# A retention layer with 64 routed experts: results scattered by token from sixteen buffers, and two projection chunks moved ahead of the routing's one-hot products

## The chip, the cores and the metric

The kernel runs on one core of a Trainium2 chip. The metric is the device time of one execution in microseconds, the median of three runs: 293.25 us (291.96 to 296.66). A profiled execution, which took 291.93 us, gives the spans and rows quoted here.

## The reference, cut to what matters

The input x is 1024 tokens of 256 channels (2 sequences of 512). The output is the sum of x, a retention layer and a mixture of experts, both of them on the normalised input.

```python
xn = _layernorm(x)
# retention: 8 heads of 32, decays g; chunk by chunk with a state
q, k, v = xn @ Wq + bq, xn @ Wk + bk, xn @ Wv + bv
inner = (q k^T * D) v ;  cross = (q * g^(i+1)) S ;  S = g^C S + (k * g^(C-1-i))^T v
# experts: 64 of width 176, six for each token; two shared ones (width 352 together)
scores = softmax(xn @ gate_w.T); topk_w, topk_ids = top_k(scores, 6); topk_w /= sum(topk_w)
routed = sum over the six of topk_w * (silu(g) * u) @ w_down[e]
shared = (silu(sg) * su) @ ws_down
out = x + retention(xn) + routed + shared
```

## The kernel before, in words

**Names.** PE multiplies matrices, ACT, DVE and POOL work on elements, SP issues plain DMAs. POOL also issues the indirect DMAs, whose rows are given by a list of indices in SBUF. P is 128, T 1024, H 256, E 64, TOPK 6.

**Stage 1, the routing (0 to 48 us).** The eight blocks of 128 tokens are normalised and transposed, the gate's logits made, and DVE marks the six chosen experts of each token (`chosen`, L753). PE ranks the tokens of each expert (L1158 to L1164). DVE splits the ranks into two digits and makes one-hot masks of them (L767, L777), of which POOL makes three of sixteen (L434). 64 small products of these masks (L1190) and eight more (L1197) give the list of tokens of each expert. PE fills its time with the projections: `q_unit` and `kv_chunk(c)`, which makes keys and values of block c by six passes (L1180). Chunks 0 to 3 stand ahead of the 64 products, chunk 4 between them and the eight, chunks 5 to 7 behind. The normalised rows and the 64 weights of each token are written to a table in DRAM.

**Stage 2, the experts (48 to 211 us).** Each expert takes a tile of 128 token slots (`TILES` is 65: the one expert with more than 128 tokens takes a second tile). For tile t:
- POOL fetches the 128 rows of the table by an indirect DMA (`gather`, L448), up to eight tiles ahead (`AHEAD`). It waits for the column of indices that DVE copies at the end of its tile (L939, `gcol`).
- SP loads the weights, 528 KB in two DMAs, into a ring of 16 slots (L361, L363). The load for expert t + 16 waits for the one two before it to land (`LOOP_PACE`).
- PE transposes the rows (L1207), multiplies by the gate and up weights in six passes (L1221), transposes the activations (L1231) and multiplies by the down weights (L1249, L1250). ACT copies the result of the tile to one of `Y_BUFS` = 8 buffers (L578), makes rounded weights (L553) and copies in between; DVE makes the rest of the rounded weights (`w_low`, L820, two operands in SBUF), the product with the routing weight (L812) and the rest of the inputs (L825).
- SP stores the tile's 128 rows to `routed` in DRAM (`store_tile`, L354), in the order: store tile t, wait for a weight load, issue the load of expert t + 16. ACT may write a buffer again when its store has landed.

Each engine runs its own instructions in order. POOL adds the bias to eight chunks of keys and values between its gathers (L474). DVE works out, from the ranks, where each token's six results lie in `routed` (`key_*`, L881 to L907).

**Stage 3, shared experts, retention and sums (211 us to the end).** When the last result is stored, POOL gathers the six rows of each token by 48 indirect DMAs of 128 rows (`gather_parts`, L457), one queue in order, five chunks ahead at most. Meanwhile PE does the shared experts (L1319, L1342) and the retention: for each block the scores (L1330), which DVE multiplies by the decay (`decayed`, L1060), and the outputs (L1372). DVE adds the six rows of a block (`sum_parts`, L1015 to L1029), then the block's output (`finish`, L1031), in a fixed order between the decays (`LAST_SUMS`), and SP stores the block (L405).

## Time and profile before

| | us |
|---|---|
| median of three runs (lowest, highest) | 293.25 (291.96, 296.66) |
| the profiled execution | 291.93 |
| its span, first to last instruction | 290.0 |
| PE, DVE, ACT, POOL busy | 251.7, 193.6, 164.3, 156.0 |
| first and last copy of a tile's result (L578) | 55.65, 210.58 |
| last product of PE, last addition of DVE | 268.6, 284.0 |

Busy shares are averages over the three stages, and say little alone: PE is over 90% busy until 268 us and idle in the last 21 us, and its row counts passes that queue behind each other. What counts is which wait ends last in each stage. The chain of work that ended last runs through DVE and PE in the first stage, through weight loads and SP in the second (41% of the span), and through POOL's 48 gathers in the third.

### The profile page before, as it was taken

To read this page: it belongs to the slowest core of one execution; us is meant where nothing else is said; L and a number is where in the kernel's file an instruction comes from. 1 tells how busy PE (TensorE), PEld (TensorE's weight loads), DVE (VectorE), ACT (ScalarE), POOL (GpSimd) and SP (SyncE) were. 2 spreads that over 40 slices of the span, in tenths; PEclk is the share of its full clock that TensorE was granted. 3 is DMA by queue.
4 is the path that set the end of the run, shared out by engine and by line. 5 is a ranking of instruction groups with operands and counts; after the bars stand their busy time and mean duration, and the time that the engine had idled before them with its cause. 6 is when DMAs were issued, how large, how long until landed. Compare 5 with 4: busy or idle time off the path is not lost.

```text
span 290.0 us, 6282 instructions
## 1 busy us (share of the span) xinstructions
PE 251.7 (87%) x1586; PEld 209.7 (72%) x1586; DVE 193.6 (67%) x476; ACT 164.3 (57%) x467; POOL 156.0 (54%) x140
## 2 busy tenths in 40 slices
PE   8978697899999999999999997889999999999000
PEld 6844485799999999999877886779744479999000
DVE  4768936878687786777665756779355469975441
ACT  1378317688887888887666756667445544241000
POOL 4296538755474554744525546311047777777750
PEclk9999979999999999999999999999999999999655
DMA  7999933999999999999889998899163333443330
GB/s 213 321 378 300 292 124 106 346 303 292 288 293 272 308 296 305 293 292 302 301 296 291 306 294 263 279 302 352 59 208 103 93 90 111 128 127 112 109 109 18
DMA packets 35302, 67.23 MB, mean 232 GB/s; under 512 B 6107, under 2 KB 22647, under 8 KB 35264
## 3 DMA queue, kind: packets, MB, share of 16 engines
q1 hardware_dynamic: 29504, 51.49, 55.4%
q0 software_dynamic: 5776, 15.48, 17.4%
q8 instruction: 10, 0.16, 0.2%
q14 instruction: 12, 0.10, 0.1%
HBM read 58.71 MB, written 12.19 MB: 244 GB/s over the span
## 4 chain that ended last, share of the span: by engine, by line
DMA 48%; POOL 15%; issue 11%; DVE 11%; PE 7%; SPq 5%; POOLq 1%; ACT 1%; DVEq 0%; ACTq 0%
DMA w_slab<-in_w 41%; POOL w_split L457 7%; SPq L361 3%; POOL early_w L457 3%; POOL digits L457 2%; DMA digits<-table,gcol 2%; DVE one_hots L767 2%; POOL end_of_ring L457 2%; DMA routed<-early_w 2%; DVE one_hots L777 1%; DMA x_slab<-in_x 1%; PE ps L1138 1%; PE ps L1221 1%; DMA w_split<-routed,key_idx 1%; DVE tab_slab L730 1%
## 5 line engine op out<-in xcount | busy, mean ns | idle before, releaser
L448 POOL DMA_INDIRECT digits<-table,gcol x65 | 71.0, 1093 | 82.3 <-DVE gcol L939 70.7
L1221 PE MATMUL ps<-w_split,xT_both 128*128 128x352 f32 x390 | 88.1, 356 | 6.5 <-ACT xT_both L559 6.3
L1221 PEld LDWEIGHTS ps<-w_split,xT_both 128*128 128x128 f32 x390 | 64.6, 189 | 18.6 <-issue 8.1
L820 DVE TENSOR_TENSOR w_split<-w_ring,w_split 128x704 fp32r<-128x704 f32 x65 | 62.5, 961 | 1.0 <-ACT w_split L553 0.5
L812 DVE SCALAR_TENSOR_TENSOR act_slab<-ps,digits,sg 128x176 f32<-128x176 f32 x64 | 25.6, 399 | 39.7 <-ACT sg L565 36.4
L553 ACT CAST w_split<-w_ring 128x704 fp32r<-128x704 f32 x65 | 51.0, 785 | 0.0
L1249 PE MATMUL ps<-w_ring,act_slab 128*128 128x256 f32 x130 | 38.9, 381 | 0.0
L1250 PE MATMUL ps<-w_slab,act_slab 128*128 128x256 f32 x130 | 38.7, 379 | 0.0
L457 POOL DMA_INDIRECT w_split<-routed,key_idx x24 | 26.1, 1087 | 7.3 <-issue 7.3
L825 DVE TENSOR_TENSOR xT_both<-ps,xT_both 128x256 fp32r<-128x256 f32 x65 | 27.0, 415 | 1.0 <-ACT xT_both L559 1.0
L1250 PEld LDWEIGHTS ps<-w_slab,act_slab 128*128 128x128 f32 x130 | 24.7, 190 | 3.3
L1207 PE MATMUL ps<-k,digits 128*128 128x128 f32 x130 | 24.8, 272 | 1.8 <-DMA digits<-table,gcol 1.1
L559 ACT CAST xT_both<-ps 128x256 fp32r<-128x256 f32 x65 | 24.2, 373 | 1.9 <-PE ps L1207 1.9
L571 ACT COPY act_slab<-ps 128x256 f32<-128x256 f32 x65 | 24.9, 383 | 0.3 <-PE ps L1231 0.3
L1231 PE MATMUL ps<-k,act_slab 128*128 128x128 f32 x130 | 24.8, 273 | 0.3 <-DVE act_slab L812 0.3
L578 ACT COPY early_w<-ps 128x256 f32<-128x256 f32 x32 | 12.0, 374 | 20.1 <-DMA routed<-early_w 11.3
L565 ACT ACTIVATE sg<-ps 128x176 f32<-128x176 f32 x65 | 20.7, 319 | 4.6 <-PE ps L1221 4.5
L578 ACT COPY y<-ps 128x256 f32<-128x256 f32 x33 | 12.3, 374 | 18.9 <-PE ps L1250 10.2
L1319 PE MATMUL ps<-xnT,sgu_sb 128*128 128x512 f32 (+1 forms) x48 | 21.2, 594 | 0.6 <-ACT y L578 0.6
L1207 PEld LDWEIGHTS ps<-k,digits 128*128 128x128 f32 x130 | 18.0, 140 | 4.1 <-DMA digits<-table,gcol 1.7
L457 POOL DMA_INDIRECT early_w<-routed,key_idx x12 | 12.9, 1076 | 14.6 <-DMA routed<-y 11.2
L1249 PEld LDWEIGHTS ps<-w_ring,act_slab 128*128 128x128 f32 x130 | 19.7, 191 | 0.1
(180 smaller groups left out, 392.0 us busy)
## 6 DMA issues: line engine op xcount, KB each, us to landing
w_ring<-in_w SPq DMA_DIRECT2D x65, 480.0 KB, 4.0
routed<-y SPq DMA_DIRECT2D x33, 128.0 KB
routed<-early_w SPq DMA_DIRECT2D x32, 128.0 KB, 4.4
w_slab<-in_w SPq DMA_DIRECT2D x65, 48.0 KB, 4.8
digits<-table,gcol POOLq DMA_INDIRECT x65, 5.1
x_slab<-in_x SPq DMA_DIRECT2D x4, 256.0 KB, 3.7
table<-tab_slab POOLq DMA_DIRECT2D x1, 1024.0 KB, 8.7
resid<-in_x SPq DMA_DIRECT2D x1, 1024.0 KB, 7.4
```

The lines of the kernel that those rows point to most:

```text
L448: pool.indirect_dma_start(out=rows[:, r, :], out_offset=None, in_=table, in_offset=bass.IndirectOffsetOnAxis(ap=gcol[:, r:r + 1], axis=0), ...
L457: pool.indirect_dma_start(out=part_sb[c % SUM_CHUNKS][:, k, :], out_offset=None, in_=routed, in_offset=bass.IndirectOffsetOnAxis(ap=key_id ...
L553: nc.scalar.copy(rr(w_hi[:, k % 4, :]), w1_sb[:, k % RING, 0:4 * F]).then_inc(whi_sb, 1)
L571: nc.scalar.copy(aT[:, k % 2, :], ps[4 + k % 2][:, 0:2 * P]).then_inc(aT_sb, 1)
L812: V.scalar_tensor_tensor(act[:, k % 2, 0:F], ps[2 + k % 2][:, F:2 * F], comb, sg[:, k % 2, :], ALU.mult, ALU.mult).then_inc(act_sb, 1)
L820: V.tensor_tensor(rr(w_lo[:, k % 2, :]), w1_sb[:, k % RING, 0:4 * F], w_hi[:, k % 4, :], ALU.subtract).then_inc(wlo_sb, 1)
L825: V.tensor_tensor(rr(xT_lo[:, k % 2, :]), ps[k % 2][:, 0:H], xT[:, k % 2, :], ALU.subtract)\
L1207: ins = nc.tensor.transpose(ps[k % 2][:, h * P:(h + 1) * P], rows[:, r, h * P:(h + 1) * P], ident)
L1221: ins = mm(ps[2 + k % 2][:, 0:2 * F], rr(a[:, k % 2, h * P:(h + 1) * P]), rr(b[:, k % (2 if b is w_lo else 4), h * 2 * F:(h + 1) * 2 * F]) ...
L1231: ins = nc.tensor.transpose(ps[4 + k % 2][:, h * P:(h + 1) * P], act[:, k % 2, h * P:(h + 1) * P], ident)
L1249: mm(ps[6 + k % 2][:, 0:H], aT[:, k % 2, 0:P], w1_sb[:, slot, 4 * F:W1C], start=True, stop=False)
L1250: mm(ps[6 + k % 2][:, 0:H], aT[:, k % 2, P:2 * P], w2_sb[:, slot, :], start=False, stop=True).then_inc(y_ps, 1)
```

## The change

- The table's rows get 32 words more: for each expert a 16 bit number, the row that the token's result for that expert has in a new DRAM tensor `parts` (token by token, six rows each). DVE makes it by a running sum over `chosen`, ACT copies it to 16 bits. A row of the gather is 1408 bytes in place of 1280.
- A tile's result isn't stored by SP, but scattered by POOL: an indirect DMA writes each valid row to its place in `parts`. DVE makes the column of indices (`scol`), one instruction for each tile. The padding slots are out of bounds, and aren't written.
- POOL's program is written out: at tile t it fetches (t up to 55), and from t = 3 on scatters one tile, except at every fourth t; at t = 56 to 59 two tiles each; then the fetch of the 65th tile, and the 17 scatters that are left.
- There are 16 result buffers, in space that is free in the expert stage.
- The final gathers, the `key_*` steps, the copies of x to `resid` and the row of zeros go. SP loads each block's six rows by one plain DMA of 768 KB, and x from the input.
- The bias of keys and values is added by DVE between tiles. `LAST_SUMS` starts two blocks later.
- PE makes chunks 4 and 5 ahead of the 64 one-hot products, chunk 6 between them and the eight, and chunk 7 behind.

```diff
-ROW = H + E
+D16 = E // 2
+ROW = H + E + D16
...
-Y_BUFS = 8
+Y_BUFS = 16
+SCATTER_LAG = 3
+SCATTER_SKIP = 4
...
-    routed = nc.dram_tensor("routed", [(TILES + 1) * P, H], f32, kind="Internal").ap()
-    resid = nc.dram_tensor("resid", [RESID_ROWS, H], f32, kind="Internal").ap()
+    parts = nc.dram_tensor("parts", [T * TOPK, H], f32, kind="Internal").ap()
...
-        y_near = sb("y", [P, 4, H])
-        y_bufs = [y_near[:, b, :] for b in range(4)] + [early_w[:, b * H:(b + 1) * H] for b in range(Y_BUFS - 4)]
-        sprod = y_near.rearrange("p (a b) h -> p a (b h)", a=2)
+        y_early = 3 * NG
+        y_bufs = [early_w[:, b * H:(b + 1) * H] for b in range(y_early)]
+        y_bufs += [tab_slab[:, b * H:(b + 1) * H] for b in range(Y_BUFS - y_early)]
+        sprod = sb("sprod", [P, 2, 2 * H])
...
-                    sp.dma_start(resid[0:T, :].rearrange("(c p) h -> p c h", p=P), x_v).then_inc(resid_done, 16)
-                    sp.dma_start(resid[T:RESID_ROWS, :], x[0:P, :]).then_inc(resid_done, 16)
-                    sp.dma_start(routed[TILES * P:(TILES + 1) * P, :], zero[:]).then_inc(zero_row_out, 16)
...
-            def store_tile(t, k, row):
-                sp.wait_ge(y_sb, t + 1)
+            def slot_free(t):
+                sp.wait_ge(y_ps, t + 1)
                 sp.sem_inc(sp_waited, 1)
-                sp.dma_start(row, y_bufs[k % Y_BUFS]).then_inc(y_out[k % Y_BUFS], 16)
 
             with sp.Fori(0, E // RING - 1) as i:
                 for s in range(RING):
-                    store_tile(i * RING + s, s, routed[bass.ds((i * RING + s) * P, P), :])
+                    slot_free(i * RING + s)
...
-            sp.wait_ge(resid_done, n_ov * 16 + 32)
+            sp.wait_ge(y_ps, n_ov + TILES)
             sp.sem_inc(sp_waited, 1)
+            sp.wait_ge(y_out[0], n_ov * 16 + y_stores(0))
+            sp.sem_inc(sp_waited, 1)
+            for b in range(1, Y_BUFS):
+                sp.wait_ge(y_out[b], y_stores(b))
+
+            def load_parts(c):
+                if c >= SUM_CHUNKS:
+                    sp.wait_ge(parts_read, c - SUM_CHUNKS + 1)
+                sp.dma_start(part_sb[c % SUM_CHUNKS], parts_v[:, c, :, :]).then_inc(parts_in[c % SUM_CHUNKS], 16)
+
+            load_parts(0)
             for n in range(2):
-                sp.dma_start(x_again[:, 4 * n:4 * n + 4, :], resid_v[:, 4 * n:4 * n + 4, :]).then_inc(x_again_in, 16)
+                sp.dma_start(x_again[:, 4 * n:4 * n + 4, :], x_v[:, 4 * n:4 * n + 4, :]).then_inc(x_again_in, 16)
+            for c in range(1, SUM_CHUNKS):
+                load_parts(c)
             for c in range(NC):
+                if c + SUM_CHUNKS < NC:
+                    load_parts(c + SUM_CHUNKS)
...
+            pool.wait_ge(dest16_ready, 1)
...
-            fetch(0, 0)
-            pool.wait_ge(kv_sb, NC)
-            pool.wait_ge(bias_in, 32)
-            with pool.Fori(0, E // RING - 1) as i:
-                for k in range(1, RING + 1):
-                    fetch(i * RING + k, k)
-                    if k in (4, 12):
-                        bias_kv(i * 2 + (k // 12))
-
-            for k in range(1, RING + EXTRA + 1):
-                if fetched_at(k) is not None:
-                    fetch(E - RING + fetched_at(k), fetched_at(k))
-                if k in (2, 4):
-                    bias_kv(NC - 3 + k // 2)
+            def scatter(t):
+                pool.wait_ge(scol_ready, t + 1)
+                pool.wait_ge(y_sb, t + 1)
+                pool.indirect_dma_start(
+                    out=parts, out_offset=bass.IndirectOffsetOnAxis(ap=scol[:, t:t + 1], axis=0),
+                    in_=y_bufs[t % Y_BUFS], in_offset=None, bounds_check=T * TOPK - 1,
+                    oob_is_err=False).then_inc(y_out[t % Y_BUFS], 16)
+
+            plain, late = E - AHEAD, E - AHEAD + LATE
+            scattered = 0
+            for t in range(late):
+                if t < plain:
+                    fetch(t, t)
+                count = 2 if t >= plain else int(t >= SCATTER_LAG and t % SCATTER_SKIP != 0)
+                for _ in range(count):
+                    scatter(scattered)
+                    scattered += 1
+            fetch(plain, plain)
+            for t in range(scattered, TILES):
+                scatter(t)
...
-            pool.wait_ge(y_ps, n_ov + TILES)
-            pool.sem_inc(pool_waited, 1)
-            pool.wait_ge(keys_ready, 1)
-            pool.wait_ge(zero_row_out, 16)
-            for b in range(Y_BUFS):
-                pool.wait_ge(y_out[b], y_stores(b))
-            for c in range(NC):
-                gather_parts(c)
...
+                if n == 3:
+                    act_e.wait_ge(dest_ready, 1)
+                    nc.scalar.copy(tab16[:, :, 2 * (H + E):2 * ROW], dest.rearrange("p (c e) -> p c e", e=E))\
+                        .then_inc(dest16_ready, 1)
...
+            dve.wait_ge(ex_ready, NC)
+            dve.wait_ge(ident_in, 16)
+            flat = chosen[:].rearrange("p c e -> p (c e)")
+            V.tensor_tensor_scan(dest, flat, flat, c_32("dest_first"), ALU.add, ALU.max).then_inc(dest_ready, 1)
...
+            def bias_kv(c):
+                part = kv[:, c, :] if isinstance(c, int) else kv[:, bass.ds(c, 1), :].rearrange("p a h -> p (a h)")
+                V.tensor_tensor(part, part, bkv_sb[:], ALU.add).then_inc(kvb_ready, 1)
...
+                if last and k >= RING:
+                    extra_dest(k % AHEAD, k - RING, link)
+                    V.scalar_tensor_tensor(scol[:, t:t + 1], ov_s[:, 5:6], -1.0, pad[:, t:t + 1], ALU.add, ALU.add)\
+                        .then_inc(scol_ready, 1)
+                else:
+                    V.scalar_tensor_tensor(scol[:, bass.ds(t, 1)], rows16[:, k % AHEAD, bass.ds(t + 2 * (H + E), 1)], -1.0,
+                                           pad[:, bass.ds(t, 1)], ALU.add, ALU.add).then_inc(scol_ready, 1)
...
-                         6: (extra_hot, 0), 7: (extra_hot_rest, 0), 8: (key_tiles, 0), 9: (key_experts, 0),
-                         10: (key_ranks, 0), 11: (key_chosen, 0), 12: (key_rows, 0)}
+                         6: (extra_hot, 0), 7: (extra_hot_rest, 0)}
...
+                    if k in (9, 17):
+                        bias_kv(i * 2 + (k // 17))
...
-                dve.wait_ge(parts_in[slot], 16 * TOPK * (c // SUM_CHUNKS + 1))
+                dve.wait_ge(parts_in[slot], 16 * (c // SUM_CHUNKS + 1))
...
-            LAST_SUMS = [[(sum_parts, 0)], [(finish, 0), (sum_parts, 1)], [(finish, 1), (sum_parts, 2)], [(finish, 2), (sum_parts, 3)],
-                         [(finish, 3), (sum_parts, 4)], [(finish, 4)], [(sum_parts, 5), (finish, 5)],
-                         [(sum_parts, 6), (finish, 6)]]
+            LAST_SUMS = [[], [], [(sum_parts, 0), (finish, 0)], [(sum_parts, 1), (finish, 1), (sum_parts, 2)],
+                         [(finish, 2), (sum_parts, 3), (finish, 3)], [(sum_parts, 4), (finish, 4), (sum_parts, 5)],
+                         [(finish, 5), (sum_parts, 6), (finish, 6)], [(sum_parts, 7), (finish, 7)]]
...
-                if n == 0:
-                    dve.wait_ge(resid_done, n_ov * 16 + 32)
-                    for b in range(Y_BUFS):
-                        dve.wait_ge(y_out[b], y_stores(b))
...
-            for c in range(4):
+            for c in range(6):
...
-            kv_chunk(4)
+            kv_chunk(6)
...
-            for c in range(5, NC):
-                kv_chunk(c)
+            kv_chunk(7)
```

PE's queue in the first stage, around the one-hot products (`one_hots`, L1190 before, L1170 now); three rows of L1180 or L1160 are half a chunk. Before:

```order
L1180 MATMUL ps<-wkv_lo,xn_hi 128x512
L1190 MATMUL ps<-one_hots 128x64 x64
L1180 MATMUL ps<-xT_both,xn_hi 128x512
L1180 MATMUL ps<-xT_both,xn_lo 128x512
L1180 MATMUL ps<-wkv_lo,xn_hi 128x512
L1180 MATMUL ps<-xT_both,xn_hi 128x512
L1180 MATMUL ps<-xT_both,xn_lo 128x512
L1180 MATMUL ps<-wkv_lo,xn_hi 128x512
L1197 MATMUL ps<-diag,k 128x64 x8
L1180 MATMUL ps<-xT_both,xn_hi 128x512
```

Now:

```order
L1160 MATMUL ps<-wkv_lo,xn_hi 128x512
L1170 MATMUL ps<-one_hots 128x64 x64
L1160 MATMUL ps<-xT_both,xn_hi 128x512
L1160 MATMUL ps<-xT_both,xn_lo 128x512
L1160 MATMUL ps<-wkv_lo,xn_hi 128x512
L1160 MATMUL ps<-xT_both,xn_hi 128x512
L1160 MATMUL ps<-xT_both,xn_lo 128x512
L1160 MATMUL ps<-wkv_lo,xn_hi 128x512
L1177 MATMUL ps<-diag,k 128x64 x8
L1160 MATMUL ps<-xT_both,xn_hi 128x512
```

The two pieces read alike, and what moved is how much stands around them: 24 passes of L1180 ahead of the 64 products before, 36 now; and behind the eight, 18 before and 6 now.

POOL's queue at the end of the experts (L448 and L464 are gathers of table rows, L457 the gathers of results, L480 the scatters). Before:

```order
L448 DMA digits<-table,gcol 128x320 x4
L492 TENSOR_LOAD ov_n
L492 ISA x2
L493 COMPARE_AND_BRANCH
L494 UNCONDITIONAL_BRANCH
L494 ISA
L497 DMA digits<-table,ov_idx 128x320
L501 REGISTER_ALU
L502 ISA
L504 DMA resid<-y,ov_idx 1152x256
L494 REGISTER_ALU
L494 COMPARE_AND_BRANCH
```

(the 48 gathers of L457 follow) and now:

```order
L464 DMA digits<-table,gcol 128x352 x2
L480 DMA parts<-early_w,scol 6144x256
L464 DMA digits<-table,gcol 128x352
L480 DMA parts<-tab_slab,scol 6144x256
L464 DMA digits<-table,gcol 128x352
L480 DMA parts<-tab_slab,scol 6144x256 x9
L464 DMA digits<-table,gcol 128x352
L480 DMA parts<-early_w,scol 6144x256 x6
L480 DMA parts<-tab_slab,scol 6144x256 x10
L480 DMA parts<-early_w,scol 6144x256
```

The first five rows are the pattern of the whole stage, three scatters for four gathers. The last gather, that of the 65th tile, now stands behind a run of nine scatters, and 17 scatters stand behind it.

## Rows read from the trace of the kernel before

**Rows 1.** A stretch: us, busy us of each engine (instructions), PEclk, DMA share, GB/s.
```profile
56.00:135.00 79.00, 79.00 (x489) 74.21 (x487) 59.02 (x142) 63.97 (x175) 42.86 (x40) 1.00 0.94 296
```

**Rows 2.** ACT in time (start, us, what, idle before <-releaser): last exponential, result copies.
```profile
21.58 0.19 ACT L533 ACTIVATION_READ_ACCUMULATOR route<-route,neg_max 128x1 f32 x1
...
55.65 0.37 ACT L578 COPY y<-ps 128x256 f32<-128x256 f32 x1 [0.44 <-PE ps L1250]
...
135.58 0.37 ACT L578 COPY y<-ps 128x256 f32<-128x256 f32 x1 [0.64 <-DMA routed<-y]
...
193.25 0.41 ACT L578 COPY y<-ps 128x256 f32<-128x256 f32 x1
...
210.58 0.37 ACT L578 COPY y<-ps 128x256 f32<-128x256 f32 x1 [0.49 <-PE ps L1250]
```

**Rows 3.** DMA issues, whole span: KB each, median us from issue to landing.
```profile
w_split<-routed,key_idx POOLq DMA_INDIRECT x24, 2.8
```

**Rows 4.** POOL in time: the first gathers, the last one, the results' gathers.
```profile
43.54 1.09 POOL L448 DMA_INDIRECT digits<-table,gcol  x1 [4.82 <-DVE gcol L793]
...
48.11 1.61 POOL L448 DMA_INDIRECT digits<-table,gcol  x1 [0.30 <-issue]
50.02 1.00 POOL L448 DMA_INDIRECT digits<-table,gcol  x1 [0.30 <-issue]
...
56.77 1.31 POOL L448 DMA_INDIRECT digits<-table,gcol  x1 [0.30 <-issue]
...
60.88 0.99 POOL L448 DMA_INDIRECT digits<-table,gcol  x1 [1.12 <-DVE gcol L939]
...
201.50 0.99 POOL L448 DMA_INDIRECT digits<-table,gcol  x1 [11.56 <-DVE gcol L939]
213.70 1.00 POOL L457 DMA_INDIRECT early_w<-routed,key_idx  x1 [11.20 <-DMA routed<-y]
...
279.48 0.99 POOL L457 DMA_INDIRECT w_split<-routed,key_idx  x1 [0.30 <-issue]
```

**Rows 5.** DVE in time: ranks, the running sum, two `w_low`.
```profile
23.09 0.69 DVE L757 SCALAR_TENSOR_TENSOR rank_i<-chosen,ps 128x512 int32<-128x512 f16 x1 [1.40 <-PE ps L1160]
...
43.52 0.34 DVE L801 TENSOR_TENSOR_SCAN ov<-ov_ones,ov 128x64 f32<-128x64 f32 x1
...
47.97 0.88 DVE L820 TENSOR_TENSOR w_split<-w_ring,w_split 128x704 fp32r<-128x704 f32 x1
...
50.05 0.90 DVE L820 TENSOR_TENSOR w_split<-w_ring,w_split 128x704 fp32r<-128x704 f32 x1
```

**Rows 6.** PE in time, around the one-hot products and at its end.
```profile
27.59 0.47 PE L1180 MATMUL ps<-xT_both,xn_hi 128*128 128x512 f32 x1 [0.87 <-ACT x_slab L543]
...
32.98 0.39 PE L1180 MATMUL ps<-wkv_lo,xn_hi 128*128 128x512 f32 x1
36.48 2.52 PE L1190 MATMUL ps<-one_hots 128*128 128x64 f16 x64 [3.12 <-DVE one_hots L777]
...
41.42 0.41 PE L1197 MATMUL ps<-diag,k 128*128 128x64 f16 x8
...
249.26 0.73 PE L1330 MATMUL ps<-x_slab,kT 32*128 32x128 f32 x16
...
267.75 0.98 PE L1372 MATMUL ps<-kv,pT 128*128 128x32 f32 x8
```

**Rows 7.** DVE in time, third stage: sums, decays, additions of outputs, the last addition.
```profile
248.34 0.95 DVE L1021 TENSOR_TENSOR act_slab<-w_split 128x768 f32<-128x768 f32 x1
...
250.59 1.28 DVE L1060 TENSOR_TENSOR pT<-ps,k 128x512 f32<-128x512 f32 x2
251.78 0.41 DVE L1034 TENSOR_TENSOR tab_slab<-w_slab,tab_slab 128x256 f32<-128x256 f32 x1
...
259.77 0.61 DVE L1104 SCALAR_TENSOR_TENSOR route<-route,k 128x128 f32<-128x128 f32 x2
...
283.58 0.43 DVE L1048 TENSOR_TENSOR tab_slab<-tab_slab,w_split 128x256 f32<-128x256 f32 x1
```

More of the change, by code:

```diff
@@ L37 @@
 UNCHOSEN = 4096.0
-SKIP = 4096
+SKIP = 8192
 SUM_CHUNKS = 5
@@ L43 @@
 _at = 0
-for _n, _w in (("ident", P), ("mask8", 8), ("padrow", 1), ("iota_e", E), ("slot_e", E), ("slot_x", E), ("iota_s", P), ("gc", NG), ("kscale", HEADS), ("qscale", NG * P), ("decay", HEADS * P)):
+for _n, _w in (("ident", P), ("dest_first", 1), ("mask8", 8), ("iota_e", E), ("iota_s", P), ("gc", NG), ("kscale", HEADS), ("qscale", NG * P), ("decay", HEADS * P)):
     C32[_n] = (_at, _at + _w)
@@ L48 @@
 C32_LATE = C32["gc"][0]
+C32_FIRST = C32["mask8"][0]
 LATE = 4
@@ L109, in build @@
         tab = view(tab_slab, 0, NC, ROW)
+        tab16 = view(tab_slab, 0, NC, 2 * ROW, dt=i16)
         x_again = view(tab_slab, 0, NC, H)
@@ L293, in build @@
         out_v = out.rearrange("(c p) h -> p c h", p=P)
-        resid_v = resid[0:T, :].rearrange("(c p) h -> p c h", p=P)
+        parts_v = parts.rearrange("(p c k) h -> p c k h", c=NC, k=TOPK)
         table_v = table.rearrange("(c p) h -> p c h", p=P)
@@ L451, in gather @@
                     bounds_check=T - 1, oob_is_err=False).then_inc(rows_in[r], 16)
-            def gather_parts(c):
-                if c >= SUM_CHUNKS:
-                    pool.wait_ge(parts_read, c - SUM_CHUNKS + 1)
-                for k in range(TOPK):
-                    pool.indirect_dma_start(
-                        out=part_sb[c % SUM_CHUNKS][:, k, :], out_offset=None, in_=routed,
-                        in_offset=bass.IndirectOffsetOnAxis(ap=key_idx[:, c * 8 + k:c * 8 + k + 1], axis=0),
-                        bounds_check=TILES * P, oob_is_err=False)\
-                        .then_inc(last_in if (c, k) == (NC - 1, TOPK - 1) else parts_in[c % SUM_CHUNKS], 16)
             pool.wait_ge(gcol_ready, 1)
@@ L606, in _ @@
                 expert_act(0, k)
-            with act_e.Fori(0, E // RING - 1) as i:
+            with act_e.Fori(0, E // RING - 2) as i:
                 for k in range(Y_BUFS + 2, RING + Y_BUFS + 2):
                     expert_act(i, k)
-            for k in range(Y_BUFS + 2, RING + EXTRA):
-                expert_act(E // RING - 1, k, ahead=min(3, RING + EXTRA - 1 - k))
+            for k in range(Y_BUFS + 2, 2 * RING + EXTRA):
+                expert_act(E // RING - 2, k, ahead=min(3, 2 * RING + EXTRA - 1 - k))
             for k in range(RING + EXTRA - 2, RING + EXTRA):
@@ L790, in indices @@
                 return V.scalar_tensor_tensor(g_out, lst, -1.0, tmp, ALU.add, ALU.add)
-            link(indices(ps[4][:, 0:E], slot_t[:], gidx[:, 0:E]))
+            link(indices(ps[4][:, 0:E], pad[:, 0:E], gidx[:, 0:E]))
             V.tensor_copy(gcol[:], gidx[:, 0:AHEAD]).then_inc(gcol_ready, 1)
@@ L871, in extra_weight, with extra_dest @@
             def extra_weight(r, n, chained):
-                chained(V.tensor_tensor(ov_comb[:], rows[:, r, H:ROW], ov_one[:, n, :], ALU.mult))
+                chained(V.tensor_tensor(ov_comb[:], rows[:, r, H:H + E], ov_one[:, n, :], ALU.mult))
                 chained(V.tensor_reduce(ov_s[:, 4:5], ov_comb[:], AX, ALU.add))
+            def extra_dest(r, n, chained):
+                chained(V.tensor_tensor(ov_comb[:], rows16[:, r, 2 * (H + E):2 * ROW], ov_one[:, n, :], ALU.mult))
+                chained(V.tensor_reduce(ov_s[:, 5:6], ov_comb[:], AX, ALU.add))
             def extra_indices(n, bank):
@@ L960, in _ @@
                     piece(n, link)
+                if k in (10, 12):
+                    bias_kv(NC - 2 + (k - 10) // 2)
             n_ov = dve.value_load(ov_n[0:1, 0:1], min_val=0, max_val=E - 1)
@@ L1114, in _ @@
                     sum_state(c + 1)
-            sum_last()
         @block.tensor
@@ L1404, in _constants @@
     a["mask8"] = (p[:, None] % 8 == np.arange(8)[None, :])
-    a["padrow"] = (T + 1 + p)[:, None]
+    a["dest_first"] = (p * NC * TOPK)[:, None]
     a["iota_e"] = np.tile(np.arange(E), (P, 1))
-    a["slot_e"] = np.tile(np.arange(E) * P + UNCHOSEN + 1, (P, 1))
-    a["slot_x"] = np.tile((np.arange(E) - (E - 1)) * P, (P, 1))
     a["iota_s"] = np.tile(np.arange(P), (P, 1))
```

84 lines of the change are left out of this document (25 added, 59 removed).

## The prediction, as it was put on record

> **What bounds the kernel now.** I read the engines' busy time by stretch first, then each stage's waits in order of time, since three stages have three limits. In the experts' stage the DMA engines are 94% busy and PE is never idle [rows 1]. Left alone, a tile takes 2.28 us: the result of tile 0 is copied at 55.65, that of tile 35 at 135.58, (135.58 - 55.65) / 35 [rows 2]. From there ACT waits for the store of the result eight tiles earlier [rows 2]: SP issues it only after weight loads have landed, so the tiles follow the DMA. Tile 56 is copied at 193.25 instead of 55.65 + 56 x 2.28 = 183.3, ten microseconds late; the last tile is copied at 210.58, 17.3 later [rows 2]. In the last stage PE ends at 268.7 [rows 6], and DVE adds until 284.0 [rows 7], because POOL issues 48 gathers one after the other from 213.70 to 279.48, 1.40 us from start to start ((279.48 - 213.70) / 47) [rows 4].
>
> **First stage.** Before the 64 one-hot products PE is idle for 3.12 us, and they wait for DVE's masks [rows 6]. Ahead of the gap 24 passes start within 27.59 to 32.98, 0.23 us apart (5.39 / 23) [rows 6]; two chunks of six passes take 2.8 us and fit into the gap. Behind the products chunk 4 kept the eight others back until 41.42, 2.42 us after the 64 ended (36.48 + 2.52) [rows 6]. At 0.23 us a pass chunk 6 takes 1.4 where chunk 4 took 2.4, so 1.0 us goes, and PE reaches the first tile two chunks sooner. Chunk 4 had passes of 0.4 us since the idle gap was followed by a lower granted clock; the 64 products should gain from that too, by at most half of their 2.52, and I take 0.6. Against this DVE's running sum over 512 columns is new. It must wait for the last exponential, 21.77 [rows 2], and DVE has room until 23.09 [rows 5]. 64 columns took 0.34 us, 512 plain ones 0.69 [rows 5]; 0.69 would cost nothing, 8 x 0.34 = 2.7 would cost 1.4. I take 1.8 in length, 0.5 in cost, between the two. Sum: the first tile starts **1.0 us earlier** (-0.4 to 2.2). The copy to 16 bits, the wider table (64 to 96 words in the second part) and the wider memset lie beside the masks, which POOL waits for anyway. The copies of x at L342 and L343, 1.1 MB, go from a time when nobody waited for them.
>
> **Experts' stage.** DMA first. A tile moved 528 KB of weights, 128 KB of stores and 96 rows on average (6144 / 64) of 1280 bytes; now 528 KB, 96 rows of 1024 and 96 of 1408: 795 to 774 thousand bytes, 2.6% less. Weights no longer stand behind stores on SP, nor the stores behind the weights. So DMA allows what it did, and with sixteen buffers the ten microseconds could come back.
>
> DVE gets one instruction of one column for a tile, shorter than the 0.34 of rows 5, and eight additions of 512 columns at 0.69 each. It is busy 75% (59.02 of 79) [rows 1], 0.57 us of each tile are free: I cost both at nothing. Without that cover they are 65 x 0.34 + 8 x 0.69 = 28 us at most.
>
> POOL is what changes. It did one indirect DMA in a tile and waited for DVE's indices (1.12 us at 60.88) [rows 4]; it also added the biases, which are gone from it. Now it does seven in four tiles. Call p the time from one to the next when POOL doesn't sleep. A scatter isn't in the trace; the nearest rows are gathers with as many rows: 1.00 us and a gap of 0.30 at best, so p = 1.30; 1.40 in the last stage; 1.47 in the start of the experts ((56.77 - 43.54) / 9) [rows 4]. The difference comes from collisions: a gather that starts inside `w_low` (48.11, in 47.97 to 48.85) has 1.61 us, until 0.87 after its end, while one that starts at 50.02, just ahead of the `w_low` of 50.05, has 1.00 [rows 4, 5]. At random phases that is (0.76 x 0.76 / 2) / 2.28 = 0.13 a piece, p = 1.43.
>
> The Trainium skill, SBUF — State Buffer, section "SBUF: two separate sides", calls the port pair of VectorE and GpSimd an exclusive lock, whoever starts first has it for the whole instruction. The trace agrees (1.61 against 1.00). By that rule p would be the 1.52 of the second rival, 6.5 us more than by the p that I take.
>
> Seven p is 9.1 at 1.30 but 10.2 at 1.45, against 4 x 2.28 = 9.1 for four tiles: POOL is the bound from about tile 3, whose fetch began at 60.88 [rows 4]. The scatters lag: by the fetch at t = 55 only 40 are done, and tile 56 writes the buffer of tile 40. That scatter starts after 53 fetches and 40 scatters, at 60.9 + 93 p, and lands 2.8 us later, as the last gathers did [rows 3], since the weights should be loaded by then. The rest takes 17.3 us as before. The fetch of the 65th tile stands eight scatters behind, 8 x 1.45 - 2.8 = 8.8 us after that landing; before it was issued at 201.50, 9.1 ahead of the last copy [rows 2, 4], which gives 17.9: I take 17.5. The last copy is at 60.9 + 93 p + 2.8 + 17.5 = 81.2 + 93 p. I take p = 1.45, the mean of 1.40, 1.43, 1.47 and the 1.52 below: 216.0, minus 1.0 of the first stage, 215.0, **4.5 us later than 210.58**. The ten microseconds of buffer waits are replaced by waits for POOL. 0.1 in p is 9.3 us: this term makes the range.
>
> **Last stage.** No gathers. 17 scatters stand behind the 65th tile's fetch, which itself is at about 206: 206 + 18 x 1.45 + 2.8 = 235. Then SP loads six rows of a block, 786 KB, and x, 1 MB: 6.2 us at 296 GB/s [rows 1], about 243 with the latency. DVE wants them 36 us after the last copy, at 251: hidden, by eight microseconds, which is the cover that is gone if POOL is 0.2 slower. The shared experts start with the last copy and keep their length, 23 us, and PE its chain in the retention. Then DVE's order decides. A decay takes 1.19 to the next instruction, a sum 2.25 (248.34 to 250.59), the addition of an output 0.41, a state sum 0.61 [rows 7]. On the clock of the old trace the scores of block 4 end at 249.26 + 0.73 = 250.0 [rows 6], and DVE has done one sum. From there it has no pause: four decays 4.8, seven sums 15.8, seven additions 2.9, two state sums 1.2, and some 0.3 for semaphores, in all 25.0, so 275.0 in place of 284.0 [rows 7]. PE waits for the last decay until 269 and ends at 270.6, which is before that. **9.0 us less** (if the parts come late 0; if DVE were free at PE's end 14). The store of 6.0 us behind it stays.
>
> **Sum.** 4.5 - 9.0 = -4.5 us (the first stage is in the 4.5). Profiled execution 291.93 to 287.4, span 290.0 to 285.5; on the median of 293.25, 1.3 above the profiled one, **288.7 us**.
>
> **The rivals.**
> - *No collisions, p = 1.30 to 1.40.* POOL falls into step with DVE, as in the loop of before, where gathers had 1.00 [rows 4]. Then POOL waits for DVE and the last copy is between the floor, 55.65 + 145 = 201, and 210: say 205 minus 1. -6.6 - 9.0: 277.7 us. For it: the phase of the loop; against: a full queue is not started by DVE, and 1.47 was measured in one.
> - *Lock step of the lock.* A gather held by `w_low` ends 0.87 after it [rows 4, 5]; the next start at 1.17, 2.47 and 3.77, the last inside the `w_low` of 3.68 to 4.56: held again. Three in two tiles, p = 4.56 / 3 = 1.52. Last copy 222.6 - 1, +11.0 - 9.0: 295.2 us, no change. For it: both collisions of the rows. Against it: slower tiles make them rarer, at 2.6 us two fit between any two.
> - *Slower, a scatter is dearer for POOL than a gather.* If it takes 1.45 with its gap of 0.30, the 40 of them cost 0.3 x 40 = 12 us more than taken: +16.5 - 9.0, 300.8 us, at the same place, the buffers that ACT waits for. It decides from 1.41 us a scatter on. No row speaks for it, and 128 rows are 128 rows; but none excludes it.
> - *The tail doesn't shrink,* since parts or DVE are late: +4.5, 297.8 us.
>
> **Chances.** The forecast (p about 1.41 to 1.50, 285 to 293) 0.42; no collisions 0.28; lock step 0.14; dear scatter 0.10; tail 0.06. A measurement here can tell 2%, 5.9 us, from no change. Below 287.4 lies p under 1.435: the first rival and 0.12 of the forecast, 0.40. Above 299.1 lies the dear scatter and a little, 0.12. Within, 0.48. Range: 278.5 to 298; below it the best of the first rival, above it the dear scatter.
>
> **What would show it.** POOL: starts of indirect DMAs in the middle of the stage 1.45 apart, scatters of 1.0 to 1.5 us; if scatters have 1.3 and more beside no `w_low`, the rival is right. ACT: no wait at the copies until about tile 40, then waits for `parts`, and the last copy at 215; if at 205 the first rival. PE: no gap ahead of the one-hot products, first gather at 42.5. DVE: no wait for parts from 246 on, last addition 69 us after the last result copy instead of 73. The forecast is wrong if POOL isn't the one whom ACT waits for, or if DVE waits for `parts` in the last stage.

## The result, and the profile after

| | before | after |
|---|---|---|
| median, us (lowest, highest; runs) | 293.41 (288.01, 300.97; 20) | 293.31 (290.83, 296.59; 20) |
| the profiled execution, its span | 291.93, 290.0 | 295.25, 293.5 |
| first, last copy of a tile's result | 55.65, 210.58 | 55.73, 226.85 |
| end of DVE's last addition | 284.0 | 291.3 |
| from there to the end of the span | 6.0 | 2.2 |

The ratio of after to before is 1.0086 (95% interval 1.0051 to 1.012). It leaves out the executions in which the chip was disturbed, while the medians hold them, and the profiled execution of the change (295.25) is one of these. The change costs about 0.9%, too little to call it slower here; 288.7 us, 1.6% less, was forecast. Three large terms cancel: the experts' stage ends 16.3 us later, the last stage is 9.0 shorter, and the end behind the last addition 3.8 shorter. 16.3 - 9.0 - 3.8 = 3.5, the difference of the spans.

ACT's copies of the results of tiles 0, 35, 56 and 64, in time, against [rows 2]:
```profile
55.73 0.38 ACT L581 COPY early_w<-ps 128x256 f32<-128x256 f32 x1 [0.44 <-PE ps L1229]
...
138.95 0.37 ACT L581 COPY early_w<-ps 128x256 f32<-128x256 f32 x1 [0.44 <-PE ps L1229]
...
209.34 0.37 ACT L581 COPY tab_slab<-ps 128x256 f32<-128x256 f32 x1 [0.44 <-PE ps L1229]
...
226.85 0.37 ACT L581 COPY early_w<-ps 128x256 f32<-128x256 f32 x1 [0.49 <-PE ps L1229]
```
Until tile 27 the tiles are 2.28 us apart as before. Then PE waits for late gathers, and from tile 38 on ACT waits for scatters. Its waits between 61 and 206 us (us in total, times, longest):
```profile
ACT tab_slab L581 <- DMA parts<-tab_slab,scol: 11.2, 8, 4.1
ACT early_w L581 <- DMA parts<-early_w,scol: 11.1, 6, 4.4
```
POOL in time: the start of its full stretch, and the last operations before the 41st scatter, which frees the buffer of tile 56; far behind, the 65th tile's fetch:
```profile
61.12 1.00 POOL L464 DMA_INDIRECT digits<-table,gcol  x1 [1.09 <-ACT early_w L581]
...
69.80 1.49 POOL L480 DMA_INDIRECT parts<-early_w,scol  x1 [0.31 <-DVE gcol L934]
...
188.27 1.02 POOL L480 DMA_INDIRECT parts<-early_w,scol  x1 [0.30 <-issue]
190.49 1.65 POOL L464 DMA_INDIRECT digits<-table,gcol  x1 [1.20 <-DVE gcol L934]
...
193.92 1.00 POOL L464 DMA_INDIRECT digits<-table,gcol  x1 [1.77 <-ACT early_w L581]
...
202.68 1.52 POOL L464 DMA_INDIRECT digits<-table,gcol  x1 [3.32 <-ACT tab_slab L581]
...
205.84 1.01 POOL L480 DMA_INDIRECT parts<-tab_slab,scol  x1 [0.30 <-issue]
...
216.98 1.39 POOL L464 DMA_INDIRECT digits<-table,gcol  x1 [0.30 <-issue]
```
Here the forecast's 93 p can be read off: (205.84 - 61.12) / 93 = 1.556 us. From 68 to 189 us POOL never sleeps (its gaps are 0.30) and needs 1.50 for each; near the end it sleeps, waiting for ACT and DVE, which wait for its scatters. A `w_low` of DVE beside the scatter of 69.80:
```profile
69.51 0.88 DVE L826 TENSOR_TENSOR w_split<-w_ring,w_split 128x704 fp32r<-128x704 f32 x1
```
The scatter starts inside it and ends at 71.29, 0.90 behind its end, as the held gather did [rows 4, 5]. Between 68 and 189 us 29 of 81 indirect DMAs start inside a `w_low` and are held (three more start in its last 0.07 us and are not); the 29 have 1.48 us on the mean, the other 52 have 1.03, scatters as gathers.

In the first stage PE's row of one-hot products, the first transposes and the passes of tiles 0 and 1:
```profile
37.09 2.04 PE L1170 MATMUL ps<-one_hots 128*128 128x64 f16 x64
...
45.69 0.41 PE L1186 MATMUL ps<-k,digits 128*128 128x128 f32 x2 [3.38 <-DMA digits<-table,gcol]
46.65 1.81 PE L1200 MATMUL ps<-w_split,xT_both 128*128 128x352 f32 x6 [0.55 <-ACT xT_both L562]
...
49.44 2.10 PE L1200 MATMUL ps<-w_split,xT_both 128*128 128x352 f32 x6 [0.55 <-ACT xT_both L562]
```
No gap ahead of the products, and 2.04 us for 2.52 [rows 6]; but a new gap of 3.38 where PE waits for the first rows, and six passes then take 1.8 to 2.1 us. The end of the trace, DVE's last addition:
```profile
290.87 0.42 DVE L1033 TENSOR_TENSOR tab_slab<-w_slab,tab_slab 128x256 f32<-128x256 f32 x1
```

### The profile page after: what moved, and what is told of

It reads as the page before. It is cut to its first block, busy times and chain, and to the rows that moved or that the text cites. A ratio compares the mean times of both kernels' runs of the same rounds, so it can differ in the third digit from the quotient of the medians.

```text
span 293.5 us, 6179 instructions
## 1 busy us (share of the span) xinstructions
PE 257.9 (88%) x1586; PEld 215.3 (73%) x1586; DVE 197.1 (67%) x537; ACT 166.5 (57%) x468; POOL 173.6 (59%) x149
## 4 chain that ended last, share of the span: by engine, by line
PE 38%; DVE 17%; DMA 16%; issue 13%; POOL 10%; ACT 4%; POOLq 0%; SPq 0%; DVEq 0%; ACTq 0%
PE ps L1200 10%; PE ps L1298 7%; DMA digits<-table,gcol 6%; DMA parts<-early_w,scol 5%; POOL parts L480 5%; POOL digits L464 5%; PE ps L1228 4%; PE ps L1229 4%; DMA parts<-tab_slab,scol 3%; PE ps L1186 3%; PE ps L1210 2%; DVE act_slab L1020 2%; DVE one_hots L773 2%; DVE pT L1045 2%; PE ps L1351 2%
## 5 line engine op out<-in xcount | busy, mean ns | idle before, releaser
L1200 PE MATMUL ps<-w_split,xT_both 128*128 128x352 f32 x390 | 90.8, 368 | 12.6 <-ACT xT_both L562 12.4
L464 POOL DMA_INDIRECT digits<-table,gcol x65 | 77.0, 1184 | 32.8 <-issue 12.5
L1200 PEld LDWEIGHTS ps<-w_split,xT_both 128*128 128x128 f32 x390 | 68.9, 199 | 22.4 <-issue 10.6
L826 DVE TENSOR_TENSOR w_split<-w_ring,w_split 128x704 fp32r<-128x704 f32 x65 | 57.4, 883 | 0.6 <-issue 0.3
L480 POOL DMA_INDIRECT parts<-tab_slab,scol x40 | 46.4, 1159 | 12.2 <-issue 10.7
L1228 PE MATMUL ps<-w_ring,act_slab 128*128 128x256 f32 x130 | 39.9, 389 | 0.0
L1186 PE MATMUL ps<-k,digits 128*128 128x128 f32 x130 | 26.2, 284 | 9.6 <-DMA digits<-table,gcol 9.5
L480 POOL DMA_INDIRECT parts<-early_w,scol x25 | 26.9, 1075 | 8.6 <-issue 6.1
L581 ACT COPY tab_slab<-ps 128x256 f32<-128x256 f32 x40 | 14.9, 374 | 27.0 <-PE ps L1229 13.6
L562 ACT CAST xT_both<-ps 128x256 fp32r<-128x256 f32 x65 | 24.2, 373 | 10.5 <-PE ps L1186 10.0
L581 ACT COPY early_w<-ps 128x256 f32<-128x256 f32 x25 | 9.3, 373 | 19.5 <-DMA parts<-early_w,scol 11.1
```

The lines of the kernel that those rows point to most:

```text
L464: pool.indirect_dma_start(out=rows[:, r, :], out_offset=None, in_=table, in_offset=bass.IndirectOffsetOnAxis(ap=gcol[:, r:r + 1], axis=0), ...
L480: pool.indirect_dma_start(out=parts, out_offset=bass.IndirectOffsetOnAxis(ap=scol[:, t:t + 1], axis=0), in_=y_bufs[t % Y_BUFS], in_offset= ...
L826: V.tensor_tensor(rr(w_lo[:, k % 2, :]), w1_sb[:, k % RING, 0:4 * F], w_hi[:, k % 4, :], ALU.subtract).then_inc(wlo_sb, 1)
L1186: ins = nc.tensor.transpose(ps[k % 2][:, h * P:(h + 1) * P], rows[:, r, h * P:(h + 1) * P], ident)
L1200: ins = mm(ps[2 + k % 2][:, 0:2 * F], rr(a[:, k % 2, h * P:(h + 1) * P]), rr(b[:, k % (2 if b is w_lo else 4), h * 2 * F:(h + 1) * 2 * F]) ...
L1228: mm(ps[6 + k % 2][:, 0:H], aT[:, k % 2, 0:P], w1_sb[:, slot, 4 * F:W1C], start=True, stop=False)
```

## The experiments

Theory 1: POOL's queue of indirect DMAs holds the result buffers, by its pace, its collisions with `w_low`, and its order. Rivals: the transfers or DVE's extra work do it (theory 2); the collisions do not matter. Two more questions came with it: what the sixteen buffers are worth (theories A and B), and why the end is 3.8 us shorter (theory E). "Copies" are ACT's result copies of tile 0 and tile 64 in the profile, p is POOL's time from start to start between 68 and 189 us (to 200 in the kernels with the new order). "Before beside it" is the median of the kernel before in the same round of runs, and the ratio is to that kernel.

| kernel | median, us | before beside it | ratio (95% interval) | copies | p |
|---|---|---|---|---|---|
| plain stores, 16 buffers | 279.34 | 294.01 | 0.952 (0.945, 0.960) | 56.4, 209.6 | |
| short `w_low` | 285.67 | 294.01 | | 56.1, 215.6 | 1.39 |
| `w_low` in halves | 288.72 | 294.01 | 0.983 (0.978, 0.988) | 55.6, 223.6 | 1.43 |
| before, 16 buffers | 291.96 | 294.01 | 0.994 (0.989, 1.000) | 55.8, 210.6 | |
| new order and halves | 280.49 | 292.74 | 0.959 (0.955, 0.962) | 56.3, 211.4 | 1.39 |
| new order alone | 285.31 | 293.16 | 0.983 (0.976, 0.991) | 56.6, 216.6 | 1.45 |
| order, halves, old chunks | 279.89 | 293.16 | 0.963 (0.955, 0.972) | 53.2, 209.5 | 1.41 |
| before, moved chunks | 293.50 | 292.74 | 1.008 (1.002, 1.015) | 56.6, 214.7 | |
| a late gather (one run) | 294.07 | 292.74 | | 55.2, 222.9 | 1.46 |
| plain stores of half rows (one run) | 274.36 | 292.74 | | 55.3, 204.4 | |
| before, last block by SP (one run) | 288.38 | 294.19 | | 56.4, 212.8 | |

The late gather runs after all copies, so that kernel is the changed one until then: its last copy at 222.9 against 226.9 shows by how much two executions can differ in this stage. So differences of up to 4 us between the last copies of two kernels, one profile of each, show nothing by themselves. Its 41st scatter:
```profile
201.80 1.01 POOL L480 DMA_INDIRECT parts<-tab_slab,scol  x1 [0.30 <-issue]
```

**The scatters taken off POOL.** SP stores each tile as before, `scatter` is not issued:
```diff
-                slot_free(i * RING + s)
+                store_tile(i * RING + s, s, parts[bass.ds((i * RING + s) * P, P), :])
...
-                for _ in range(count):
-                    scatter(scattered)
```


> The changed kernel with its results stored by SP as in the kernel before: one plain store of a tile from each of the sixteen buffers, no scatter on POOL. The sums at the end read rows that belong to other tokens, so what is computed after the routed experts is not the reference's; sizes and counts stay. DVE still writes its column of destinations for each tile. Theory 1 (POOL's queue of two indirect DMAs a tile holds the result buffers): POOL has 65 gathers only, ACT never waits for a buffer, PE not for gathers; tiles 2.28 us apart, last result copy at 55.7 + 64 x 2.28 = 201.6, at most 206, instead of 226.9; then the 66.3 us of the changed kernel's last stage: span 268 to 272, time 270 to 274. Theory 2 (DVE's extra column and biases, or the memory traffic, set the pace of the experts' stage): the last copy stays at 220 or later, time above 286.


Measured: no wait for a buffer, last copy 17.2 us earlier, time 279.34 (270 to 274 was expected). DVE kept its extra column and its biases, so theory 2 falls: POOL's scatters cost the 17. But the last copy is at 209.6, not 201.6:
```profile
136.00 0.37 ACT L577 COPY early_w<-ps 128x256 f32<-128x256 f32 x1 [0.44 <-PE ps L1225]
...
209.63 0.37 ACT L577 COPY early_w<-ps 128x256 f32<-128x256 f32 x1 [0.49 <-PE ps L1225]
```

**Sixteen buffers in the kernel before.** `Y_BUFS = 16`, the new ones in `early_w` and `tab_slab`.


> The kernel before with sixteen result buffers instead of eight and nothing else: stores stay on SP, the 48 gathers on POOL. Theory A (the waits of ACT for stores were a matter of buffers): no wait at ACT's result copies, last copy at 202 to 205 instead of 210.6, the gathers of the last stage start so much earlier, time 285 to 288. Theory B (the DMA engines are the limit of this stage and the waits only showed it): the last copy at 208 or later, time 291 to 294.


Measured: ACT's waits from 150 to 211 us no longer name the stores, and name the weights instead:
```profile
ACT w_split L556 <- DMA w_slab<-in_w: 8.3, 12, 1.7
```
The last copy is at 210.57, where it was with eight buffers [rows 2]. Theory B holds: the ten microseconds of waits were the late weights, seen at the buffers. The ratio, 0.994, is at most a per cent of gain. The weights were bound to be late: from 56 to 135 us the kernel before issues 28 loads of weights,
```profile
w_ring<-in_w SPq DMA_DIRECT2D x28, 480.0 KB, 3.9
```
one in 2.8 us (79 / 28), while PE does a tile in 2.28 [rows 2] and so uses up what was loaded ahead. This could have been estimated beforehand: the prediction's 795 thousand bytes of a tile at the 296 GB/s of [rows 1] are 2.69 us.

**The same limit from its other side.** The kernel with plain stores, half of each stored:
```diff
-                sp.dma_start(row, y_bufs[k % Y_BUFS]).then_inc(y_out[k % Y_BUFS], 16)
+                sp.dma_start(row, y_bufs[k % Y_BUFS][0:P // 2, :]).then_inc(y_out[k % Y_BUFS], 16)
```


> The kernel with plain stores by SP from sixteen buffers in which only half of each result, 64 rows of 128, is stored (the sums read one block of rows again and again, so the output is not the reference's). Theory B (the bytes through the DMA engines set the last sixteen tiles, where PE waits for weights): 64 KB of some 774 in a tile less, the stretch from 56 to 210 us is up to 8% of it shorter, last copy at 201 to 204 instead of 209.6. Rival (the issue of the weights behind the landing of earlier ones on SP sets it, not the bytes): last copy stays at 208 to 210.


Measured: 204.42, just outside the 201 to 204 of theory B, at 8% fewer bytes 5.2 us earlier, 4.1 of it behind the first copy. A pure limit by bytes would give 0.081 x 153.2 = 12.4, of which PE's own 64 x 2.27 = 145.3 us allow 7.9: the stretch is 149.1 us, it was 153.2. This is one run, and 4 us is what two executions of one kernel differed by, so it only leans to theory B. Nor does it part the bytes from SP's order, in which a load waits for an earlier one to land: from 56 to 135 us 29 loads were issued in place of 28, and the DMA engines moved 277 GB/s in place of 293, so they did not stay at one rate. `LOOP_PACE` was not varied.

**A `w_low` too short to collide with.**
```diff
+                cols = 4 * F if isinstance(t, int) and t < 2 else 64
-                V.tensor_tensor(rr(w_lo[:, k % 2, :]), w1_sb[:, k % RING, 0:4 * F], w_hi[:, k % 4, :],
+                V.tensor_tensor(rr(w_lo[:, k % 2, 0:cols]), w1_sb[:, k % RING, 0:cols], w_hi[:, k % 4, 0:cols],
```


> The changed kernel in which DVE's subtraction for the low part of the weights covers 64 columns instead of all from the third tile on (the rest of the low part is that of the first two tiles, so the products are not the reference's); all waits, DMAs and PE passes stay. Theory 1 (a third of POOL's indirect DMAs start inside this subtraction and are held until it ends, 0.15 us a piece over all): POOL's pace in the full stretch falls from 1.50 to about 1.35, last result copy 93 x 0.15 = 14 us earlier, at about 213 instead of 226.9, time about 279. Rival (the collisions are there but POOL's time is set by waits for landings and for DVE and ACT): pace stays near 1.5, last copy after 222, time 290 or more.


Measured: 6 of 86 operations start inside it and none of them takes more than 1.06 us, p falls to 1.39, the last copy comes at 215.6, 11.2 earlier (14 was named) and the median is 285.67 (279 was named). The rest came back as sleep:
```profile
186.80 1.02 POOL L480 DMA_INDIRECT parts<-tab_slab,scol  x1 [0.31 <-issue]
192.01 1.02 POOL L464 DMA_INDIRECT digits<-table,gcol  x1 [4.19 <-DVE gcol L935]
```
POOL is then faster and sleeps more: its order holds it.

**`w_low` in two halves,** which computes the same:
```diff
+                for part in (slice(0, 2 * F), slice(2 * F, 4 * F)):
+                    ins = V.tensor_tensor(rr(w_lo[:, k % 2, part]), w1_sb[:, k % RING, part], w_hi[:, k % 4, part],
```


> The changed kernel with DVE's subtraction for the low part of the weights made in two instructions of half the columns. Theory 1 (an indirect DMA is held only until the one instruction ends in which it starts): the hold is half as long, 0.07 us less on the mean of all, last result copy about 93 x 0.07 = 6.5 us earlier, near 220, time about 287. Rival (a held DMA loses both halves, as the second follows at once): longest durations stay at 1.7 us, no gain, time 293 to 294.


Measured: the mean of the colliding ones falls from 1.48 to 1.20, p to 1.43, the time to 288.72, 4.6 under the change. Most are held for one half only, some for both (1.76 was seen). The last copy, at 223.6 where 220 was expected, is from an execution of 292.05 us, 3 above the median, and says less than the time does.

**Another order of POOL's queue.**
```diff
-LATE = 4
+LATE = 2
...
-                count = 2 if t >= plain else int(t >= SCATTER_LAG and t % SCATTER_SKIP != 0)
+                count = int(t >= SCATTER_LAG and (t % SCATTER_SKIP != 0 or t >= 34))
```


> The changed kernel with DVE's subtraction in two halves, and with another order of POOL's queue: from the 35th tile on each fetch is followed by a scatter (before, none after every fourth), so that 45 scatters and not 40 are done by the fetch of t = 55, and the 65th tile's fetch stands behind two more scatters, not eight. Theory (POOL's order costs sleep: fetches run ahead of need while ACT waits for scatters, and POOL then waits for ACT and DVE): the last copy comes after 57 fetches and 47 scatters at 1.43 us without sleep, 61 + 104 x 1.43 = 210, plus 8 to 10 us = 218 to 220 instead of 223.6, and POOL sleeps under 2 us between 68 and 205; time 283 to 285. Rival (the sum of POOL's work alone counts, the order does not): last copy at 223 to 224, time 288.7 as with the halves alone.

> The changed kernel with the new order of POOL's queue alone (each fetch followed by a scatter from the 35th tile on, 45 scatters done by the fetch of t = 55, the 65th tile's fetch behind two more), DVE's subtraction in one piece. Theory (sleep and order were the larger part of what the halves and the order gave together, 280.5 against 293.3): p stays near 1.50, as the collisions are back, 104 operations behind 61 without sleep end at 217, last copy at 218 to 221 against 226.9, time 285 to 288. Rival (the collisions are the larger part, the order does little without the halves): last copy at 224 or later, time 291 or more.


Measured: with the halves 280.49 and the last copy at 211.4 (283 to 285 and 218 to 220 were expected), alone 285.31 and 216.6 (expected 285 to 288 and 218 to 221). In both, no wait of POOL is longer than 0.6 us between 68 and 206, where in the change three cost it 5.4 us beyond its gaps of 0.30. New order with halves, the same place as above:
```profile
193.11 1.13 POOL L464 DMA_INDIRECT digits<-table,gcol  x1 [0.30 <-issue]
194.55 1.02 POOL L480 DMA_INDIRECT parts<-tab_slab,scol  x1 [0.31 <-issue]
195.88 1.12 POOL L464 DMA_INDIRECT digits<-table,gcol  x1 [0.30 <-issue]
...
201.22 1.22 POOL L464 DMA_INDIRECT digits<-table,gcol  x1 [0.30 <-issue]
```
The 65th tile's fetch starts at 201.2 instead of 217.0, the last copy is at 211.4, within 2 us of the limit that the weights set. ACT's waits for scatters between 61 and 206 us are 4.8 us instead of 22.3:
```profile
ACT early_w L581 <- DMA parts<-early_w,scol: 3.6, 5, 0.9
ACT tab_slab L581 <- DMA parts<-tab_slab,scol: 1.2, 2, 0.6
```
Order alone is worth 8.0 us, halves alone 4.6, both 12.8 (medians, against 293.31): they add. Which is worth more isn't settled: by the ratios, each to the kernel before beside it, both have 0.983 and together 0.959, where the change has 1.009.

**The chunks of keys and values.** First in the kernel before, moved (its one edit); then in the best kernel, moved back:
```diff
-            for c in range(4):
+            for c in range(6):
```


> The kernel before with the order of PE alone changed: chunks 4 and 5 of keys and values ahead of the one-hot products, 6 and 7 behind them. Forecast of the prediction for this part: first gather at about 42.0 to 42.5 instead of 43.54 and the first result copy 1.0 us earlier, at 54.6. Rival (PE now stands idle for over 3 us until the first rows land and its passes after it are at a lower granted clock): the first gather comes 1 to 1.5 us earlier, the first result copy at 55.5 to 55.9. Either way the last copy at 209.5 to 210.6, since the transfers set it, and the time within 1 us of the kernel before.

> The changed kernel with DVE's subtraction in halves, the new order of POOL's queue, and PE's order of the chunks of keys and values as in the kernel before (four ahead of the one-hot products, then 4, then 5 to 7). Theory (the chunks moved ahead leave PE idle for over 3 us until the first rows land, and the clock falls over the first tiles): first gather 1 us later, at 43.5, first result copy at 55.7 or earlier, and since DMA sets the last copy, the time is 279.5 to 280.5, no more than 1 us under the 280.5 with the moved chunks. Rival (the moved chunks do give their 1.0 us): time 281 to 282.


Measured in the kernel before with moved chunks: first gather at 42.42, 1.1 us earlier [rows 4]; first result copy at 56.62, 1.0 us later [rows 2], later still than the rival's 55.5 to 55.9. The last copy is at 214.7 and not at 209.5 to 210.6, and the ratio of 1.008 (1.002 to 1.015) is some 2.5 us, where at most 1 was expected. Whether the new gap costs that in later tiles, or two executions just differ so, no run shows. PE's passes of tile 0, and the stretch (columns as in [rows 1]):
```profile
46.71 2.10 PE L1220 MATMUL ps<-w_split,xT_both 128*128 128x352 f32 x6 [0.55 <-ACT xT_both L559]
```
```profile
46.00:52.00 6.00, 4.89 (x17) 4.26 (x17) 2.85 (x5) 2.49 (x6) 4.56 (x5) 0.50 0.79 241
```
The granted clock is 0.50, the lower level of 1.2 GHz, behind 3.3 us in which PE waited for the first rows. With the chunks moved back in the best kernel:
```profile
46.38 1.27 PE L1203 MATMUL ps<-w_split,xT_both 128*128 128x352 f32 x6 [0.55 <-ACT xT_both L562]
```
```profile
46.00:52.00 6.00, 4.73 (x28) 3.92 (x29) 4.66 (x15) 3.87 (x10) 4.47 (x6) 1.00 0.81 269
```
The full clock, and the first copy at 53.17, better than I expected; yet the first gather stays at 42.17, since here the clock did not fall ahead of the 64 products either (a gap of 2.87 us, before 3.12) and chunk 4 was fast. In all nine kernels with the moved chunks the clock was 0.50 to 0.60 from 46 to 52 us, in the four with the old order 1.00. The end gains little, as the weights set the last copy: 279.89 and 280.49 are not told apart.

**The end behind the last addition.** A gather added to the change behind the last addition but one, and six taken from the kernel before:
```diff
+            pool.wait_ge(res_sb, 7)
+            pool.indirect_dma_start(
...
-            for c in range(NC):
-                gather_parts(c)
+            for c in range(NC - 1):
+                gather_parts(c)
```


> The changed kernel with one more gather on POOL, into rows that nobody reads, that waits for the last addition but one (288.5 us on the clock of the trace) and is issued at about 289; it lands before 293. Theory E (the end of the program waits some 9.5 us after POOL's last indirect DMA: 280.5 to 290.0 in the kernel before, 280.3 to 289.9 with sixteen buffers): the span ends 9.5 us after this gather's end, at about 299 to 300 instead of 293.5. Rival (what follows the last addition is the store and nothing else, and the 3.8 us more of the kernel before have another cause): the span stays at 293.5.

> The kernel before, in which the six rows of the eighth block's parts do not come by POOL's last six gathers but by two plain loads of SP from other rows (so the eighth block of the output is not the reference's). POOL's last gather starts 6 x 1.3 = 7.8 us earlier, at about 271.7, and DVE does not wait for it. In the kernel before, with sixteen buffers, and with the moved chunks the span ended 10.5, 10.6 and 10.6 us after the start of POOL's last gather, and 6.0, 6.1 and 6.1 us after DVE's last addition, which waited for that gather, so that these do not tell the two apart. Theory E (the end is bound by POOL, 10.5 us after the start of its last gather, or by 2.2 us after the last addition, whichever is later): DVE's last addition ends at 276 to 280, the span at 282.2 or 2.2 after the addition. Rival (the gathers on POOL make the end cost 6.0 us after the last addition wherever they stand): the span ends 6.0 us after the last addition, 282 to 286.


Measured with the late gather: it starts at 285.35 (I had misjudged the addition it waits for), the last addition ends at 287.31, and the span at 292.3, 5.0 us behind it instead of 2.2. Neither side is right as put: the rival wanted 2.2 us behind the addition, theory E 9.5 behind the gather's end, where there are 5.9. With the last block by SP, POOL's last gather and DVE's last addition:
```profile
272.40 1.00 POOL L467 DMA_INDIRECT w_split<-routed,key_idx  x1 [0.30 <-issue]
```
```profile
283.96 0.42 DVE L1058 TENSOR_TENSOR tab_slab<-tab_slab,w_split 128x256 f32<-128x256 f32 x1
```
The span ends at 286.6, 2.2 behind the addition, where it was 6.0. So the rival falls: the 3.8 us belong to POOL's last gathers, and the kernel before was bound at its end by POOL and not by DVE. The addition itself ended at 284.4 and not at 276 to 280: the last copy of this execution was late, at 212.75, and without the waits for gathers DVE waited four times, 2.0 to 3.6 us, for scores of PE. The 10.5 us from POOL's last gather are not a constant: the late single gather took 7.0.

## Why the prediction was wrong, step by step

- **First stage, -1.0 us: the start right, the gain not.** The first gather came at 42.53, as forecast. DVE's running sum took 1.28 us (taken 1.8) and moved the ranks from 23.09 to 23.52 [rows 5]. But the gap that the moved chunks filled came back behind them, and the clock fell there: the first result copy is 0.08 us later, not 1.0 earlier. The step "PE reaches the first tile two chunks sooner" failed, since PE reached only a wait sooner.
- **Sixteen buffers "could" bring ten microseconds: they could not.** No term of the sum, but the floor of 201 under the first rival. With 16 buffers and no POOL limit the last copy is at 209.6 to 210.6, because the weights come in 2.8 us apart. "The tiles follow the DMA" stood in the prediction; that this stays so with more buffers did not.
- **Experts' stage, 81.2 + 93 p: the failed step.** POOL was the bound, for the buffer of tile 56, and the rest behind it took 17.5 as put. The last copy is 11.8 us later than the 215.0. Of that 1.2 is the later start (61.12 for 60.9 - 1.0), 93 x 0.04 = 3.8 a p of 1.49 awake instead of 1.45, 0.7 a longer landing, and 6.1 the sleep that the formula has no term for: 93 p with p "when POOL doesn't sleep" takes it that POOL never does. It does sleep: at t = 52, 53 and 55 (5.4 us, the rest at t = 5) the fetch waits for DVE and ACT, which wait for scatters that stand only a few places ahead of it in the same queue and have not landed. Order alone took the sleep away and 8.0 us of time. The other execution of the same program (the late gather) shows that this is the step, and not the size of p: there the 93 operations take 60.66 to 201.80, the sleep is 6.8, and what is left is 1.44 for each, the 1.45 of the forecast; its last copy, at 222.9, is 7.9 late.
- **The rivals.** Not "no collisions": 29 of 81 collide. The lock step comes nearest: it gives one held of three and 1.52, and 29 of 81 are held and p is 1.50. But the holds come in no fixed step (two in a row, five free), and in the other execution it is 21 of 82 and 1.46, so the traces do not tell it from chance; the 3.8 us are all that it explains. Here the lock of the port pair, as the Trainium skill states it (SBUF — State Buffer, "SBUF: two separate sides"), agrees with the traces on the single hold: 0.90 us from the end of `w_low`, and a short `w_low` leaves 1.04 a piece. The other half of that rule, that the one who starts second is blocked whoever it is, does not show: 31 `w_low` of the changed kernel start while an indirect DMA runs on POOL, between 61 and 206 us, and each takes 0.88 to 0.91, as the one of 50.05 did within the gather of 50.02 [rows 4, 5]. So the prediction's "the trace agrees" held for one direction. Not the dear scatter: 1.03 us beside no `w_low`, 1.41 was its threshold.
- **Last stage, -9.0 us: right.** Last addition 64.1 us behind the last copy's end, 73.1 before (the prediction's sign, "69 us", does not follow from its own sum, which gives 275.0 - 210.6 = 64.4 behind the last copy's start, and 64.4 it was); the parts are loaded from 244.9 on, and first summed at 263.5. The same 64.1 stands in every kernel with this last stage.
- **"The store of 6.0 us behind it stays": wrong by 3.8 us.** That was POOL's queue and went with the gathers. It hid a third of the miss: +11.8 - 3.8 = 8.0, the span of 293.5 against 285.5.

## What to carry to other kernels

A queue whose work is a sum of operations is only as good as its order: where an operation waits in the end for others that stand only just ahead of it, the queue sleeps while it is the bound, so place each by when its result is wanted, not by an even pattern. Before buffers are added, look what the producer waits for behind them: the wait moves to the next late thing. And moving filler work ahead of a gap moves the gap; it pays only if nothing else waits at the new place.
